# Mix stage: banded row sums, packed triangles, and x's two fp16 parts transposed by DMA instead of on TensorE

## The reference

```
x = _layernorm(x + _L0_gnn_ref(x, adj, ...))     # similarity over all slabs, 153 best neighbours
x = _layernorm(x + _L1_gnn_ref(x, adj, adj, ...))
x = _layernorm(x + _L2_gnn_ref(x, adj, W_lang, W_grav, ...))   # the mix stage
x = _layernorm(x + _L3_gnn_ref(x, adj, ...))     # the same algorithm as L0

def _L2_gnn_ref(h, mask, W_lang, W_grav, W_V, W_O, gate, log_sigma):   # h: (64, 128, 512)
    z_l, z_g, v = h @ W_lang.T, h @ W_grav.T, h @ W_V.T
    A_l = relu(cosine similarity of the rows of z_l), A_g = exp(-distance^2 of the rows of z_g / 2 sigma^2)
    K = w_l * normalised(A_l * mask) + (1 - w_l) * normalised(A_g * mask)
    return (K @ v) @ W_O.T
```

## Time and profile before

| | us |
|---|---|
| median of three runs | 1514.57 (1511.9 to 1514.67) |
| the profiled execution, device time | 1517.64 |
| its span, first to last instruction | 1516.1 |
| PE busy in the span | 1369.1 (90%) |
| DVE busy | 1127.5 (74%) |
| ACT busy | 850.0 (56%) |
| POOL busy | 562.2 (37%) |

### The profile page before, as it was taken

How to read it: one execution, slowest core, us unless ns; L and a number is a source line. 1 busy time by engine, 2 the same in 40 slices (tenths; PEclk the granted TensorE clock), 3 DMA queues, 4 the chain that set the end, 5 groups by cost and what they waited for, 6 DMA issues and landing times. The chain is left out here.

```text
span 1516.1 us, 31781 instructions
## 1 busy us (share of the span) xinstructions
PE 1369.1 (90%) x9432; PEld 772.6 (51%) x9432; DVE 1127.5 (74%) x2235; ACT 850.0 (56%) x1396; POOL 562.2 (37%) x845
## 2 busy tenths in 40 slices
PE   6689969999999699999999999999937992899997
PEld 2255545555555265555555555555513652455554
DVE  0498777888888468777777777777767877666665
ACT  4634435777777445555555555555443432577786
POOL 0100135778788202222222222222231001488887
PEclk9899978999999799999999999999978995899999
DMA  9656100000000000000000000000004530022222
GB/s 328 246 174 203 53 8 1 1 0 0 0 0 0 1 1 2 1 0 0 0 0 0 0 0 0 0 0 0 1 1 138 189 119 1 28 77 83 81 78 97
DMA packets 39341, 72.47 MB, mean 48 GB/s; under 512 B 4112, under 2 KB 4240, under 8 KB 39296
## 3 DMA queue, kind: packets, MB, share of 16 engines
q1 hardware_dynamic: 39200, 71.78, 13.7%
q0 software_dynamic: 96, 0.13, 0.0%
HBM read 54.86 MB, written 17.04 MB: 47 GB/s over the span
## 5 line engine op out<-in xcount | busy, mean ns | idle before, releaser
L519 PE MATMUL pair<-unit_lo,unit_hi 128*128 128x512 f16 x512 | 178.3, 386 | 25.7 <-ACT unit_hi L565 22.2
L1727 POOL TENSOR_TENSOR sq_lo<-sq,sq_hi 128x512 f16<-128x512 f32 x60 | 69.5, 1158 | 224.9 <-ACT sq_hi L1497 224.9
L565 ACT ACTIVATE unit_hi<-kept 128x512 f16<-128x512 f32 x128 | 79.4, 630 | 120.6 <-DVE kept L543 75.4
L523 PE MATMUL diag<-unit_hi 128*128 128x128 f16 x512 | 113.3, 221 | 0.0
L521 PE MATMUL pair<-unit_hi 128*128 128x384 f16 (+2 forms) x384 | 106.2, 277 | 0.0
L543 DVE TENSOR_TENSOR kept<-x_all,sim 128x512 f32<-128x512 f32 x128 | 81.2, 685 | 26.0 <-DMA sim<-rn_rows 24.4
L1241 POOL TENSOR_TENSOR x_all<-x_all,t 128x512 f32 (+1 forms) x64 | 81.4, 1271 | 47.4 <-ACT t L1145 39.7
L1068 PE MATMUL po<-an_h,xwh 128*128 128x512 f16 x256 | 98.0, 383 | 0.0
L1069 PE MATMUL po<-an_l,xwh 128*128 128x512 f16 x256 | 98.0, 383 | 0.0
L1070 PE MATMUL po<-an_h,xwl 128*128 128x512 f16 x256 | 97.8, 382 | 0.0
L1273 PE MATMUL po<-an_h,xwh 128*128 128x512 f16 x256 | 97.5, 381 | 0.0
(11 more groups left out here) (378 smaller groups left out, 4298.3 us busy)
## 6 DMA issues: line engine op xcount, KB each, us to landing
sim<-rn_rows SPq DMA_DIRECT2D x128, 256.0 KB, 3.5
x_all<-in_x_dram SPq DMA_DIRECT2D x16, 1024.0 KB, 14.5
out_dram<-x_all SPq DMA_DIRECT2D x64, 256.0 KB, 2.0
weights_a<-in_L_gnn_W_lang_dram SPq DMA_DIRECT2D x1, 1024.0 KB, 12.3
weights_b<-in_L_gnn_W_grav_dram SPq DMA_DIRECT2D x1, 1024.0 KB, 8.3
weights_a<-in_L_gnn_W_O_dram SPq DMA_DIRECT2D x1, 1024.0 KB, 10.5
an_h<-in_L_gnn_W_V_dram SPq DMA_DIRECT2D x1, 512.0 KB, 6.0
an_l<-in_L_gnn_W_V_dram SPq DMA_DIRECT2D x1, 512.0 KB, 8.4
```

The lines of the kernel that those rows point to most:

```text
L519: nc.tensor.matmul(pair[i][:], stat, lo[:, r, :], start=first, stop=False, skip_group_check=True)
L523: last = nc.tensor.matmul(diag[:, i * P:(i + 1) * P], stat, stat, start=(first and i == 0), stop=final, skip_group_check=True)
```

## The change

In words: (1) `norm_sums` now runs once in a step, at its end, for all four slabs of group i-2. The bank is split into four bands of 32 rows, slab j of a group goes to band j, and the stationary tile is 128 x 32 (`pick`, copied by POOL once in a group). The squares of a group have tiles of their own (`sq_hi`, `sq_lo` with `G` slots). (2) PE's 32 transposes and the four PSUM copies go. SP issues two DMA transposes in each step, one for the high and one for the low part of the four slabs (128 x 2048 fp16, 512 KB each), into `xT`, of which there are now two. (3) `xs` has no tile of its own any more: its parts lie in `tl_hi` and `tl_lo`, the tiles of the W_lang projection. (4) The weights' triangles are stored packed. (5) The fourth layer takes its slabs with the bands' order: 60 rows of scales are early and 4 late, stored with four DMAs each, where it was one of 32 rows each.

```diff
+    tail = total - ahead - (total - ahead - head) % ring
...
+            self.rows = slice(0, P)
+            runs = [(slice(j * BAND + 1, j * BAND + RUN), slice(G + j, B, G)) if early else
+                    (slice(j * BAND, j * BAND + 1), slice(j, j + 1)) for j in range(G)]
...
+def triangle(d, cs):
+
+    at = sum(N - r * P for r in range(d)) - d * P
+    return slice(at + cs.start, at + cs.stop)
...
-        xs = k.sb(ctx, "xs", [P, 2, G, N], F16)
-        xT = k.sb(ctx, "xT", [P, C, 2, N], F16)
+        xT = [k.sb(ctx, f"xT{r}", [P, 2, G, C, P], F16) for r in range(2)]
+        xs = (tl_hi, tl_lo)
...
+                def transposes(s):
+                    g, slot = s.at(0), s.slot(0)
+                    need(sp, v_d, (g - 1) * G)
+                    for h, ready in enumerate((xs_hi, xs_lo)):
+                        settle(sp, ready, (g + 1) * G, k.idle["sp"])
+                        sp.dma_start_transpose(out=xT[slot][:, h].rearrange("p j d t -> p (j d) t"),
+                                               in_=xs[h][:].rearrange("p j n -> p (j n)")).then_inc(xt_in, 16)
+                pipeline(sp, NG, 0, 2, transposes)
                 early.store(sp)
...
-                def transposes(g):
-                    pe.wait_ge(xs_lo, (g + 1) * G)
...
-                def project(g, w_h, w_l, free, done):
+                def project(g, slot, w_h, w_l, free, done):
...
+                            need(pe, v_l, (g - 1) * G + e + 1)
+                            if e == 0:
+                                pe.wait_ge(xt_in, 32 * (g + 1))
...
-                def norm_sums(s, j):
...
+                def norm_sums(g):
+                    if last_group(g):
                         pe.wait_ge(early.clamped, 1)
+                    pe.wait_ge(pick_r, g + 1)
+                    pe.wait_ge(sq_l, (g + 1) * G)
+                    for part in range(2):
+                        for j in range(G):
+                            last = nc.tensor.matmul(rows_bank[j * BAND:(j + 1) * BAND, :], pick[:], square_tiles(g, j)[1 + part],
...
-                    if not last_group(b):
-                        need(act, ns_d, b)
+                    if not last_group(g):
+                        need(act, ns_d, g * G)
...
-                        need(act, v_d, g * G)
-                        for d in range(0, C, 2):
-                            act.wait_ge(t_d, g * C + d + 1)
-                            nc.scalar.activation(xT[:, d, :, :].rearrange("p h n -> p (h n)"), work[d][:].bitcast(F16),
...
                         need(act, gl_d, g)
+                        act.wait_ge(xt_in, 32 * (g + 1))
...
-                pipeline(pe, NG, 2, 1, step, ahead=1)
+                pipeline(pe, NG, 2, 2, step, ahead=1)
...
+                        need(pool, ns_d, g * G)
+                        pool.tensor_copy(pick[:], unit_col[:, bass.ds(g, BAND)]).then_inc(pick_r, 1)
```

More of the change, by code:

```diff
@@ L88, in pipeline @@
         step(Step(i, i % ring, total))
-    with strided(eng, head, total - ahead, ring) as base:
+    tail = total - ahead - (total - ahead - head) % ring
+    with strided(eng, head, tail, ring) as base:
         for j in range(ring):
             step(Step(base + j, j % ring, total))
-    for i in range(total - ahead, total + depth):
+    for i in range(tail, total + depth):
         step(Step(i, i % ring, total))
@@ L1362, in _ @@
             def _(pe):
-                def transposes(g):
-                    pe.wait_ge(xs_lo, (g + 1) * G)
[L1365 to L1372, removed]
-                def project(g, w_h, w_l, free, done):
+                def project(g, slot, w_h, w_l, free, done):
+                    xT_h, xT_l = xT[slot][:, 0], xT[slot][:, 1]
                     for e in range(C):
@@ L1377, in project, with gram @@
                             pe.wait_ge(free, g * C + e + 1)
[L1378 to L1381, removed]
+                        else:
+                            need(pe, v_l, (g - 1) * G + e + 1)
+                            if e == 0:
+                                pe.wait_ge(xt_in, 32 * (g + 1))
+                        to = grouped(work[e][:], G)
                         for d in range(e + 1):
[L1383 to L1386, removed]
+                            block = triangle(d, slice(e * P, (e + 1) * P))
+                            nc.tensor.matmul(to, w_h[:, block], columns(xT_h, d), start=(d == 0), stop=False)
+                            nc.tensor.matmul(to, w_h[:, block], columns(xT_l, d), start=False, stop=False)
+                            last = nc.tensor.matmul(to, w_l[:, block], columns(xT_h, d), start=False, stop=(d == e))
                         last.then_inc(done, 1)
-                def gram(bank, t_h, t_l, done):
+                def gram(slot, bank, t_h, t_l, done):
+                    xT_h, xT_l = xT[slot][:, 0], xT[slot][:, 1]
                     for j in range(G):
@@ L1403, in norm_sums @@
                         pe.wait_ge(early.clamped, 1)
[L1404 to L1407, removed]
-                    nc.tensor.matmul(rows_bank[:], pick, hi, start=first, stop=False, skip_group_check=True)
-                    nc.tensor.matmul(rows_bank[:], pick, low, start=False, stop=final,
-                                     skip_group_check=True).then_inc(ns_d, 1)
+                    pe.wait_ge(pick_r, g + 1)
@@ new lines, in norm_sums @@
+                    pe.wait_ge(sq_l, (g + 1) * G)
+                    for part in range(2):
+                        for j in range(G):
+                            last = nc.tensor.matmul(rows_bank[j * BAND:(j + 1) * BAND, :], pick[:], square_tiles(g, j)[1 + part],
+                                                    start=(isinstance(g, int) and g == 0 and part == 0),
+                                                    stop=(last_group(g) and part == 1), skip_group_check=True)
+                    last.then_inc(ns_d, G)
@@ L1709, in step @@
                         early.refine(dve)
-                pipeline(dve, NG, 2, 1, step, ahead=1)
+                pipeline(dve, NG, 2, 2, step, ahead=1)
             @block.gpsimd
```

156 lines of the change are left out of this document (72 added, 84 removed).

## The result

The changed kernel takes 1471.31 us, the median of 4 runs (1470.76 to 1472.06), beside 1514.62 us for the kernel before on the same chip (4 runs). The ratio is 0.9718, with a 95% interval from 0.9701 to 0.9735. The change gains 43.3 us; 34.6 were forecast.

What follows compares the result with a forecast made beforehand. PE bounds the mix stage before; afterwards the chain between grams over DVE, POOL and ACT, at 34.9 us a step. Terms -36 + 3.4 - 2.0 = -34.6 us give 1480.0 us, range 1465 to 1535.

Steps and rivals of the forecast that it cites:

- the slack: Mix stage's steady steps: PE waits some 0.9 us a step for the chain, which would cover two tiling-mode drains.
- the transposes are hidden: Mix stage: xT ready 13.3 us after the gram, needed at 18.8; no steady cost. With the chain bounding, chance 0.62.
- the term of the stage's start: Mix stage's start: group 0 has no cover for its DMA transposes, cost 3.4 us.
- D: Time one 512 KB DMA transpose occupies SP's queue: 4.4 us, from plain copies landing after 6.0 less 1.6 latency.
- the lower bound: Least queue time of one DMA transpose: 1.7 us, at the loading stretch's 312 GB/s.
- the rivals with late transposes: Mix stage: transposes late by a little (0.07, 1491 to 1511 us) or becoming the bound, slower (0.21).
- the third rival: Transposes late by a little, D between 7.1 and 8: period 34.9 to 36.6, total 1491 to 1511 us; chance 0.07.
- the steady term: Mix stage's steps: period from 37.32 to 34.9 us, 2.4 us a step over 15 distances, gain 36 us.
- the chain tightens too, PE bounds: Rival for the mix stage's steps: DVE's and ACT's waits shrink, gain 45 to 51 us, 1463 to 1474; chance 0.08.
- the end: Mix stage's end: last product no longer waits behind the third slab's sums; net gain 0.1 to 2, taken as 2.0 us.
- the likeliest case: The forecast itself: transposes hidden, chain bounds the mix stage; 1474 to 1491 us, chance 0.62.
- case 1: Mix stage: transposes hidden, chain bounds; -24 to -41 us, 1474 to 1491; chance 0.62.

Runs made afterwards that it cites:

- the two edits that shorten it: Changed kernel with squares one place later in ACT's and POOL's lists: 1465.93 us; changed kernel with DVE's mix-stage list written out instead of looped: 1467.06 us.
- serial sums: Changed kernel with a 128-column stationary tile for the row sums, so that the eight matmuls pass one after another: 1484.24 us, ratio 0.9814.
- the squares later: Changed kernel with each square of x one place later in ACT's list and its low part in POOL's: 1465.93 us, ratio 0.9683.

## Why the prediction came out as it did

**Right: what bounds it, before and after.** PE was the limit before. With 37.32 - 34.12 = 3.2 us less work a step it isn't in the looped steps: they stop at the chain, 0.5 us above PE's own time, where 0.9 were forecast. The chain's links in the changed kernel, from these rows of the DVE, POOL and ACT timelines:

```profile
780.13 0.18 DVE L1694 BATCH_NORM_AGGREGATE mv<-bn 128x2 f32<-128x6 f32 x1
780.61 0.38 POOL L1753 TENSOR_SCALAR rs<-mv 128x4 f32<-128x4 f32 x1 [3.17 <-DVE mv L1694]
782.78 0.23 POOL L1759 TENSOR_SCALAR rs<-rs 128x4 f32<-128x4 f32 x1 [0.20 <-POOL rs L1757]
783.21 2.94 ACT L1521 ACTIVATE x_all<-x_all,rs  x4 [1.43 <-POOL rs L1759]
792.72 0.46 DVE L1636 TENSOR_TENSOR small<-small,rnl 128x4 f32<-128x4 f32 x1
793.75 0.14 DVE L1639 TENSOR_SCALAR small<-small 128x4 f32<-128x4 f32 x1
795.64 1.13 DVE L1651 SCALAR_TENSOR_TENSOR gs<-es,small,gs 128x128 f32<-128x128 f32 x4
```

The gram of the language weights ends at 765.35. To DVE's statistics it is 780.31 - 765.35 = 15.0 (forecast 15.2), to POOL's end 2.7 (2.7), to ACT's start 0.2 (0, a hand-over that I left out), to DVE's combination 796.77 - 783.21 = 13.6 (13.9), K's transpose and the gram 3.2 (3.1). These add up to the step, 34.64 us, as they must; forecast were 34.9. ACT's normalisation now waits for POOL and for nothing else, as said. That the chain is the cause is shown by the two edits that shorten it, each in another link.

**Right: the bands.** Eight sums 0.54 us, forecast 0.6, and 1.04 us more where they are serial. Four do go at a time. The pauses at a change of tile size, which the prediction left to the slack, are there, some 0.25 us a step; 0.1 of them lie in the 0.54 and the rest makes PE's step 34.12 us where 34.0 was forecast. The slack covers them in the nine looped steps only, and in the others they are paid. The new addresses of weights and `xT` cost nothing: with serial sums the step is 35.16 us, and the kernel before gives 33.43 + 1.73 = 35.16.

**Right: the transposes are hidden, and one alone waits.** They need 2.9 + 7.0 = 9.9 us from the gram, of some 18.5 that there are.

**Mis-sized: the term of the stage's start, +3.4, measured 0.0.** The step at fault is D = 4.4, "the same size and issuer with the least company", taken from a load out of HBM. A transpose from SBUF to SBUF occupies the queue for 2.5 us, 0.8 us longer than the lower bound and far from the upper one. My 1.6 us for latency fits: 2 x 2.5 + 1.6 = 6.6 against 7.0 us. Of the two figures of the Trainium skill, that of "DMA: Bandwidth & Descriptors", Latency and other measured facts, was the near one: an effective 261 GB/s, where some 210 were reached here, and the measurement decides. The 1309 ns per block of "VectorE: DVE Perf Modes", The three transpose paths, don't add up over the 16 blocks of one DMA: both parts, 32 blocks, moved in 5 us, 0.16 us a block. With the measured D, the rivals with late transposes, 0.28 of the chance, lose their ground: they begin at D = 7.1. (The lower bound of the third rival is also added up wrongly: at D = 7.1 its own terms give 15 x (34.8 - 37.32) + 8.8 - 2 = -31, thus 1484 us and not 1491.)

**Mis-sized: the steady term, -36, measured -41.8** (-1.9 and -39.9). Two causes. First, the 13.9 us from ACT to DVE's combination held a stretched instruction whose length depends on when it falls. In the kernel before, the fourth of DVE's small pieces met POOL's low part of a square; these are the rows of that collision, from the DVE and POOL timelines of the kernel before:

```profile
818.24 0.18 DVE L1638 RECIPROCAL small<-small 128x4 f32<-128x4 f32 x1
818.34 0.80 DVE L1639 TENSOR_SCALAR small<-small 128x4 f32<-128x4 f32 x1
...
817.95 1.17 POOL L1727 TENSOR_TENSOR sq_lo<-sq,sq_hi 128x512 f16<-128x512 f32 x1 [3.17 <-ACT sq_hi L1497]
```

L1639 lasts 0.80 us and ends at 819.14, POOL's instruction at 819.12; in the changed kernel it lasts 0.14, while L1636 has 0.46 instead of 0.15. So (0.80 + 0.15) - (0.14 + 0.46) = 0.35 us of the chain hung on where that meeting fell. That is what this link lost, 13.88 - 13.56 = 0.32 us, and about the difference between 34.9 and 34.64. The nine looped distances gain 2.7 us each, 24.2 together where 21.6 were forecast. Second, I multiplied one looped step by 15. In the others a part of DVE's list is written out, and there its dependent instructions follow one another sooner. The larger share is in the first link: behind the gram at 1007.32 us the statistics end 13.6 us later (1020.75 + 0.18), in the loop 15.0. The small pieces ahead of the combination add to it: from L1636's start to L1646's 1067.40 - 1066.15 = 1.25 us, in the loop 794.85 - 792.72 = 2.13, of which 0.3 are the meeting with POOL. So the chain is short enough, and PE is the limit at 34.12 or so: five of them gain 14.8 us, forecast 12, and the last one 0.85, forecast 2.4. That makes -39.9. The other 1.9 come in the first, incomplete step, which loses PE's transposes too and which I hadn't counted. The rival "the chain tightens too, PE bounds" is thus true of those steps, though not for its reason (DVE's and ACT's waits for PE), and becomes true of all with one small edit.

**Right: the end.** -2.2 us, forecast -2.0.

That the two errors point the same way is why the time lies 8.7 us under the forecast, 3 us below the likeliest case's own range (1474) and within the whole one. It lies in the range that the prediction gave to that rival, 1463 to 1474. (By that rival's own terms, -45 to -51 with a start of +8.2 to -2.0 and an end of 0 to -2.7, the range is 1459 to 1478 and overlaps with case 1's.) The whole time alone could therefore not have told the two cases apart; PE's wait in nine steps does.

## What to carry to other kernels

Where one engine is busy all the time, add up the next chain from rows before counting work taken off that engine as gain: here 3.2 us a step left PE and 2.7 came out, and the last half microsecond was to be had only by an edit to the chain itself, to ACT's and POOL's order or to DVE's loop. Look in that sum for instructions that last several times as long as their likes, and for the steps that are written out rather than looped, since the sum of a looped step holds for the loop alone. A transpose of 512 KB inside SBUF by DMA takes 2.5 us of the queue and 4.5 to 4.9 us to land; with 18 us of other work on PE two of them a step cost nothing here, and they free PE, ACT and DVE.

## What the runs showed of the hardware

- Matmuls with 32-column stationary tiles, each in a band of its own and all into one PSUM bank, go four abreast: the first four of a group start together and the next four 0.22 us later, and the eight of 512 columns take 0.54 us, where eight with a 128-column tile took 1.73. The changes of tile size before and after them cost some 0.25 us together.
- A small DVE instruction and POOL's 128x512 `sq_lo` meet in all ten traces, in nine or more of the 16 steps, and the DVE one ends with POOL's, within 0.04 us. Which one it is depends on where POOL's falls: L1636 in the changed kernel, L1639 in the one before, L1640 (the same instruction) with the squares later, L1641 with DVE's list written out, there with 1.07 us. In the kernel with both parts transposed twice the two rows, from the DVE and POOL timelines, are:

```profile
742.59 0.99 DVE L1639 TENSOR_TENSOR small<-small,rnl 128x4 f32<-128x4 f32 x1
742.41 1.16 POOL L1731 TENSOR_TENSOR sq_lo<-sq,sq_hi 128x512 f16<-128x512 f32 x1 [2.67 <-ACT sq_hi L1514]
```

  They end at 743.58 and 743.57. Its twin in the kernel before (L1636, at 817.63) lasts 0.15 us. The Trainium skill, "GPSIMD Engine Reference", Specifications, says that GpSimd shares its SBUF interfaces with VectorE and that DVE instructions with two SBUF inputs contend for them. This instruction has two, and the rows agree; the one in the kernel before (L1639, `small<-small`) has one. The same row of that page also names a 2-port perf mode, and whether L1639 runs in one no trace here shows. The reciprocal ahead of it (L1638), which has one input too, starts at 818.24 within the same POOL instruction and keeps its 0.18 us. No run moved POOL's instruction alone, so the cause is argued, not shown. The two edits to the chain did not work by ending this meeting: in both of them it lasts longer (1.02 and 1.07 us) than in the changed kernel (0.46).
- Reading `xT` in four runs of 128 columns and the packed triangles cost nothing that the step shows (35.16 us with serial sums, as the kernel before's parts add up to).
- The same DVE list is slower as a loop: 15.0 us from the gram to the statistics looped, 13.6 written out, on the same operations in the same order.
